# One core, moving-average attention and routed FFN: five half-width jobs made neighbours, steps of copies and stores changed, a sigmoid computed by tanh

## What is computed

```python
def attention(xn):                  # p, a = sigmoid(delta), sigmoid(alpha)
    q = 1 - p * a                   # two decays per feature
    kernel = sum over 2 of p * beta * gamma * (1/2)**0.5 * q**t
    return silu(causal_convolution(xn, kernel) + xn * omega)

def ffn(xn):                        # R = 4 rounds, E = 4 experts, top 2
    cur = xn
    for r in range(4):
        logits = cur @ Wg[r] + bg[r]
        w = softmax of the two highest logits, 0 for the two others
        y_e = gelu(cur @ W1[e] + b1[e]) @ W2[e] + b2[e]      # hidden width 512
        cur = cur + sum_e w_e * y_e
    return cur
```

## Time and profile before

| | us |
|---|---|
| median of 3 executions (lowest, highest) | 658.93 (656.51, 660.35) |
| the profiled execution, its own time | 661.23 |
| its span, first to last instruction | 659.4 |
| PE busy | 604.5 (92%) |
| ACT busy | 515.5 (78%) |
| DVE busy | 474.2 (72%) |
| POOL busy | 395.6 (60%) |
| mean granted clock of TensorE | 0.975 of full speed |

### The profile page before, as it was taken

One profiled execution on the slowest core, in us unless ns is written; L12 is line 12 of the kernel. 1 busy time (PEld: TensorE's weight loads), 2 busy tenths in 40 slices (PEclk: granted clock), 3 DMA queues, 4 the chain that ended last, 5 costly groups with the idle time before them and its releaser, 6 DMA issues.

```text
span 659.4 us, 11311 instructions
## 1 busy us (share of the span) xinstructions
PE 604.5 (92%) x3308; PEld 503.1 (76%) x3308; DVE 474.2 (72%) x1080; ACT 515.5 (78%) x984; POOL 395.6 (60%) x412
## 2 busy tenths in 40 slices
PE   7989999989999999999899999999999999889991
PEld 7767887868877788778787888788877787668780
DVE  4996966588967887559955787659865897647671
ACT  5879688868887789778877888878877788758770
POOL 5665276362875368534864368535868877687154
PEclk8989999989999999999989999999999999989996
DMA  9202033635987489665985589667977688767940
GB/s 243 79 3 64 2 100 105 225 152 219 337 283 254 190 294 351 217 220 225 329 281 210 192 315 347 193 225 271 328 252 266 238 298 303 243 236 282 343 171 32
DMA packets 73754, 146.97 MB, mean 223 GB/s; under 512 B 9383, under 2 KB 37214, under 8 KB 73694
## 3 DMA queue, kind: packets, MB, share of 16 engines
q1 hardware_dynamic: 67396, 134.12, 57.9%
q0 software_dynamic: 5824, 11.87, 5.6%
q10 hardware_dynamic: 474, 0.28, 0.2%
HBM read 37.42 MB, written 12.09 MB: 75 GB/s over the span
## 4 chain that ended last, share of the span: by engine, by line
PE 53%; POOL 15%; DVE 10%; DMA 7%; issue 6%; ACT 4%; SPq 2%; POOLq 0%; DVEq 0%; ACTq 0%
PE z L1479 8%; PE y L1499 7%; PE z L1485 7%; PE z L1482 7%; PE y L1501 7%; PE y L1500 7%; POOL sorted_rows L820 7%; PE spare L1401 5%; DMA w_job<-w_all 4%; POOL state L806 4%; POOL out_dram L837 3%; DVE h_lo L1298 2%; PE misc L1423 2%; ACT z L956 2%; DVE weighted L1226 2%
## 5 line engine op out<-in xcount | busy, mean ns | idle before, releaser
L1298 DVE TENSOR_TENSOR h_lo<-z,h_hi 128x512 fp32r<-128x512 f32 (+1 forms) x432 | 250.0, 592 | 108.1 <-ACT h_hi L959 104.5
L956 ACT ACTIVATE z<-z,w_job 128x512 f32<-128x512 f32 (+1 forms) x368 | 212.9, 579 | 78.4 <-PE z L1485 66.5
L959 ACT CAST h_hi<-z 128x512 fp32r<-128x512 f32 (+1 forms) x432 | 221.8, 513 | 13.7
L806 POOL TENSOR_TENSOR state<-state,weighted 128x512 f32<-128x512 f32 (+1 forms) x90 | 107.0, 1189 | 106.3 <-DVE weighted L1226 105.2
L1479 PE MATMUL z<-cur_hi,w_job 128*128 128x512 f32 (+2 forms) x368 | 138.7, 377 | 6.1 <-DMA w_job<-w_all 5.1
L820 POOL DMA_INDIRECT sorted_rows<-rows,position_i x112 | 115.4, 1031 | 37.0 <-issue 20.9
L1499 PE MATMUL y<-h_hi,w_job 128*128 128x512 f32 (+1 forms) x368 | 131.5, 357 | 4.1 <-DVE h_lo L1298 4.0
L1482 PE MATMUL z<-cur_lo,w_job 128*128 128x512 f32 (+2 forms) x368 | 129.3, 351 | 0.0
L1485 PE MATMUL z<-cur_hi,w_job 128*128 128x512 f32 (+2 forms) x368 | 129.3, 351 | 0.0
L1500 PE MATMUL y<-h_lo,w_job 128*128 128x512 f32 (+1 forms) x368 | 128.9, 350 | 0.0
L1501 PE MATMUL y<-h_hi,w_job 128*128 128x512 f32 (+1 forms) x368 | 128.7, 350 | 0.0
(11 more groups left out here) (165 smaller groups left out, 785.4 us busy)
## 6 DMA issues: line engine op xcount, KB each, us to landing
w_job<-w_all SPq DMA_DIRECT2D x92, 514.5 KB, 3.9
w_job<-w_all SPq DMA_DIRECT2D x92, 512.0 KB, 4.0
gate_bc<-gate_rows SPq DMA_DIRECT2D x71, 256.0 KB
rows<-sorted_rows SPq DMA_DIRECT2D x28, 266.0 KB, 4.3
gate_bc<-gate_rows SPq DMA_DIRECT2D x37, 128.0 KB
out_dram<-x_tok SPq DMA_DIRECT2D x8, 256.0 KB, 5.6
sorted_rows<-rows,position_i POOLq DMA_INDIRECT x112
rows<-in_L_ffn_W_dram SPq DMA_DIRECT2D x4, 256.0 KB, 7.5
```

What stands on the lines that cost most here:

```text
L806: pool.tensor_tensor(state[job.g][:, cols_at], before, weighted[:, j % TR, 0:job.n], ALU.add).then_inc(added, 1)
L956: nc.scalar.activation(zs, zs, ACT.Gelu_apprx_tanh, bias=bias).then_inc(gelu_done, 1)
L959: nc.scalar.copy(h_hi[:, s % ZR, 0:job.n], zs).then_inc(hi_act, 1)
L1298: dve.tensor_tensor(h_lo[:, s % ZR, 0:job.n], zs, hs.bitcast(F32), ALU.subtract).then_inc(lo_done, 1)
```

## The change

1. `SORTED_JOBS`: X3 and X4 stand ahead of F4, so that the five short jobs are fifth to ninth in phases 1 to 6, as they are in phase 7 already.
2. Steps in `SORTED`: transposes, copies and logits around the phase's end, the scatters, the table's parts, the attention parts of the first batch in phases 1 and 2. In `BEFORE_LAST` the stores of group 0.
3. The sigmoids of delta and alpha are 0.5 tanh(0.5 v) + 0.5: ACT's tanh stands behind its first step, the exponential and DVE's reciprocal are gone. The dummy gelu stands first on ACT.
4. ACT's copy of batch 0 out of `spare` stands behind step 0; expert 2's first high part is made by POOL.

```diff
-SORTED_JOBS = "F0 F1 F2 F3 X0 X1 X2 F4 X3 X4 F5 F6 F7".split()
+SORTED_JOBS = "F0 F1 F2 F3 X0 X1 X2 X3 X4 F4 F5 F6 F7".split()
...
-    "P": (42, 45, 51, 53), "P copy": (46, 48, 55, 57), "P split": (44, 46, 49, 55),
-    "P logits": (46, 53, 54, 57), "I": (46, 52, 56, 59), "I copy": (49, 55, 59, 62),
-    "I split": (47, 56, 59, 63), "G": 48, "G copy": 52, "ema": (22, 25, 27, 30, 34, 36), "ema tanh": 36,
-    "A": 41, "A add": 42, ...
-    "places": (17, 18), "pairs": (21, 22), "order": 21, "pick": 28, "jobs": 28, "table": 37,
-    "scatter": (18, 18, 18, 19, 19, 19, 20, 20, 25, 25, 29, 31, 33, 35, 39, 42), "ema 2": (0, 1, 2, 3, 4, 6),
-    "ema tanh 2": 6, "A 2": 7, "A add 2": 10}
+    "P": (42, 44, 51, 53), "P copy": (46, 48, 53, 57), "P split": (44, 46, 49, 55),
+    "P logits": (46, 51, 54, 57), "I": (46, 52, 55, 59), "I copy": (49, 55, 59, 62),
+    "I split": (47, 56, 59, 63), "G": 49, "G copy": 52, "ema": (22, 25, 27, 30, 34, 36), "ema tanh": 36,
+    "A": 39, "A add": 41, ...
+    "places": (17, 18), "pairs": (22, 22), "order": 21, "pick": 27, "jobs": 31, "table": 35,
+    "scatter": (19, 20, 20, 20, 21, 23, 24, 24, 25, 27, 31, 33, 35, 35, 40, 42), "ema 2": (2, 3, 4, 5, 6, 9),
+    "ema tanh 2": 8, "A 2": 11, "A add 2": 14}
...
-    "P add": (43, 46, 53, 57), "finish": (48, 50, 54, 60), "idents": -1,
+    "P add": (43, 46, 53, 57), "finish": (45, 48, 55, 60), "idents": -1,
...
-                    split_weights(e, second, 2 * e + second > 4)
+                    split_weights(e, second, e >= 2)
...
+            act.wait_ge(consts, 2)
+            nc.scalar.activation(warm[:], ident[:, 0:1], ACT.Gelu_apprx_tanh)
             split_weights_hi(0)
             split_weights_hi(1)
-            act.wait_ge(ema_coef_in, 16 * 2)
-            nc.scalar.activation(ema_e[:], ema_in[:, 0:2, :], ACT.Exp, scale=-1.0).then_inc(ema_exp, 1)
-            act.wait_ge(consts, 2)
-            nc.scalar.activation(warm[:], ident[:, 0:1], ACT.Gelu_apprx_tanh)
...
-            act.wait_ge(w1_in[2], 16)
-            nc.scalar.copy(w_all[:, 2, 0:F], w1_raw[:, 2]).then_inc(w_hi, 1)
-            from_spare(("N", 0))
...
+                    if s == 0:
+                        from_spare(("N", 0))
+                        act.wait_ge(ema_coef_in, 16 * 2)
+                        nc.scalar.activation(ema_s[:], ema_in[:, 0:2, :], ACT.Tanh, scale=0.5).then_inc(ema_tanh, 1)
...
-                dve.tensor_scalar(ema_s[:], ema_e[:], 1.0, None, ALU.add).then_inc(ema_chain, 1)
+                dve.tensor_scalar(ema_e[:], ema_s[:], 0.5, 0.5, ALU.mult, ALU.add).then_inc(ema_chain, 1)
                 dve.wait_ge(ema_chain, 1)
-                dve.reciprocal(ema_e[:], ema_s[:]).then_inc(ema_chain, 1)
```

More of the change, by code:

```diff
@@ L118 @@
 SORTED = {
-    "P": (42, 45, 51, 53), "P copy": (46, 48, 55, 57), "P split": (44, 46, 49, 55),
-    "P logits": (46, 53, 54, 57), "I": (46, 52, 56, 59), "I copy": (49, 55, 59, 62),
-    "I split": (47, 56, 59, 63), "G": 48, "G copy": 52, "ema": (22, 25, 27, 30, 34, 36), "ema tanh": 36,
-    "A": 41, "A add": 42, "gates": (7, 8, 8, 10), "tanh": 13, "weights": 15, "count": 16, "ranks": 15,
-    "places": (17, 18), "pairs": (21, 22), "order": 21, "pick": 28, "jobs": 28, "table": 37,
-    "scatter": (18, 18, 18, 19, 19, 19, 20, 20, 25, 25, 29, 31, 33, 35, 39, 42), "ema 2": (0, 1, 2, 3, 4, 6),
-    "ema tanh 2": 6, "A 2": 7, "A add 2": 10}
+    "P": (42, 44, 51, 53), "P copy": (46, 48, 53, 57), "P split": (44, 46, 49, 55),
+    "P logits": (46, 51, 54, 57), "I": (46, 52, 55, 59), "I copy": (49, 55, 59, 62),
+    "I split": (47, 56, 59, 63), "G": 49, "G copy": 52, "ema": (22, 25, 27, 30, 34, 36), "ema tanh": 36,
+    "A": 39, "A add": 41, "gates": (7, 8, 8, 10), "tanh": 13, "weights": 15, "count": 16, "ranks": 15,
+    "places": (17, 18), "pairs": (22, 22), "order": 21, "pick": 27, "jobs": 31, "table": 35,
+    "scatter": (19, 20, 20, 20, 21, 23, 24, 24, 25, 27, 31, 33, 35, 35, 40, 42), "ema 2": (2, 3, 4, 5, 6, 9),
+    "ema tanh 2": 8, "A 2": 11, "A add 2": 14}
 DENSE_PHASE = {
@@ L429, in ema_and_routed_ffn_kernel @@
         wg_ready = sem("wg_ready")
-        ema_exp = sem("ema_exp")
+        ema_tanh = sem("ema_tanh")
         ema_chain = sem("ema_chain")
@@ L1240, in attention @@
                     if c == 0:
-                        dve.wait_ge(ema_chain, 7)
+                        dve.wait_ge(ema_chain, 6)
                     dve.tensor_scalar(pre[:], here, omega_half[:], None, ALU.mult).then_inc(ema_step, 1)
```

7 lines of the change are left out of this document (3 added, 4 removed).

## The result

| | before | changed |
|---|---|---|
| median, us (lowest, highest) | 659.39 (656.51, 660.35), 4 executions | 651.24 (650.07, 651.67), 4 executions |
| profiled execution, span | 659.4 | 649.7 |
| PE busy | 604.5 | 602.8 |
| mean granted clock | 0.975 | 0.981 |

The ratio is 0.9881, with a 95% interval of 0.9847 to 0.9915: faster by 8.1 us, where 10.3 were forecast (648.6 us, range 640 to 657). A second series on another chip gave 651.69 against 658.23 us, ratio 0.9891 (0.9847 to 0.9935).

The account below looks back on a forecast made before the run. PE, busy 604.5 of 659.4 us, was taken as the bound, so gains come only from its idle time and low-clock stretches. Waits removed, less +5.6 for the short jobs and +0.6, summed to -10.3 us: 648.6 us, range 640 to 657.

Parts of the forecast that it names:

- Copies at the phase's end: Starts of phases 2 to 6: PE's five waits on ACT's copies go, -5.8 us, bounds 0 and -5.8.
- End of the dense phase: Later scans give PE its block 2.1 us earlier, leaving a 0.6 us wait without low clock: -3.0 us.
- First batch's attention: Transpose waiting for ACT stands four steps later, -0.7 us; its last DVE part behind the gates costs +0.6.
- State and sorted rows: PE's short waits on X4's add go, -1.4 us; waits on rows read back go if steps between lengthen, -2.5.
- End of phase 6: Wait of 3.66 us on POOL's add goes, wait on x_tok grows from 1.0 to 2.4: -2.3 us.
- Start: ACT reaches its first gelu sooner, so gates from DVE come earlier for PE: -0.8 us, bounds 0 and -1.5.
- Five short jobs in a row: Steps 16 to 40, phases 1 to 6: late weights raise 146.5 to 152.1 us, +5.6; bounds 139.8 and 159.
- The pairs and tables: Pairs, pick, jobs and table parts move among steps with the same DVE work before the same matmul: nothing.
- rival 4: Waits for weights of 1.87 us or more bring low clock in each of six phases: 663.9 us, chance 0.06.
- Rivals 2 and 3: 2: weights come in time, 638.8 us, chance 0.12. 3: PE's waits on ACT's copies move on, 654.4 us, chance 0.15.
- Rival 1: The run of short jobs costs its upper bound, 159 us for steps 16 to 40: 655.5 us, chance 0.15.
- the signs that were named: Predicted PE waits after the change, steps 16 to 40 at 25 to 26 us; wrong if w_job waits exceed 12.

Follow-up runs that it names:

- e9: Kernel before with only the copy of block 2 at step 53 (from 55) and logits of block 1 at 51 (from 53); 654.79 us, ratio 0.9918.
- e10: Changed kernel with an eighth of the weight bytes copied for the five short jobs and F4; 641.88 us, ratio 0.9725; serves for times alone.
- e11: Changed kernel with old job order, block 2's transpose at 56, two gathers at 13 and 14, earlier register loads, first P transposes a step later; 647.87 us, ratio 0.9787.
- e6: Changed kernel with the old order of jobs (F4 between X2 and X3), all table steps as changed; 648.08 us, ratio 0.9855.
- e12: e11 with the last two gathers of phase 6's start at steps 43 and 44 instead of 13 and 14; 645.37 us, ratio 0.9778.
- e4: Changed kernel with the transpose of the next phase's block 2 at step 56 (from 55); ratio 0.9701 on a chip with slower transfers.
- e8: Changed kernel with F4's to F6's register loads read earlier, block 2's transpose at step 56, two phase 6 gathers at 13 and 14; 645.80 us, ratio 0.9831.
- e5: The changed kernel itself again, on another chip; 651.69 us, ratio 0.9891.

## Why the prediction held, and where not

**Copies at the phase's end, -5.8.** Right. All five waits went. e9 measures 4.5 us for it alone (5.4 by the ratio, with an interval of 3.5 to 7.4), and 1.0 us came back there on POOL's adds and 1.0 in phase 6. In the changed kernel, where X4's add comes earlier, nothing comes back on the adds: steps 0 to 8 of phases 2 to 6 lose 2.3 us each and F6 and F7 gain 0.95 in phases 1 to 5, -6.7 together.

**End of the dense phase, -3.0.** Steps 0 to 8 of phase 1 went from 17.43 to 14.34 us (-3.1), and 0.7 of it came back in steps 8 to 16 (10.03 to 10.72), 0.44 of that with the transpose of the first batch's attention, which moved there: -2.4. The low clock is gone. The wait forecast at 0.6 is 1.67, so the step that was wrong is how soon PE starts behind the add. Where it started at once, in e10 and e11, the wait was 0.8 and steps 0 to 8 took 13.5 us, 0.9 less than here.

**First batch's attention, -0.7 and +0.6.** Phase 2 lost 3.65 us in steps 0 to 8 where the phases behind it lost 2.3, and 0.44 came back in steps 8 to 16, again the transpose itself: -0.9. The cost on DVE did not appear.

**State and sorted rows, -1.4 and -2.5.** Both lines are gone from PE's waits. e6 shows the cause for the first: with the old order and the new tables the adds are waited for again, 3.4 us without the dense phase's end. So the order of jobs pays here, not the steps of the scatters. For the second the reason given was wrong: it was to go only if the steps between took longer, yet in e6 they take 146.9 us, as before, and of the 2.5 us only 0.2 are left. PE waits for the adds there instead. In e11 and e12, where the transposes of `P` stand a step later, the waits on the adds are gone and those on the rows are 3.3 and 4.3 us. With the old order one or the other was left in each of these runs. Steps 40 to 52 fell by 2.8 us although 4.7 came in with the logits (0.95 in five phases) and 2.7 of transposes went out; so their waits fell by 4.8, where the two terms had 3.9.

**End of phase 6, -2.3.** The 3.66 us are gone as forecast, but the wait on `x_tok` is 3.12 and not 2.4, since DVE's add to `state` ahead of it takes 1.64 us, where before it took 0.91, and the low clock follows. Steps 0 to 8 of phase 7 fell from 19.99 to 18.21 us: -1.8. It is the transpose at step 55 that costs: with it at 56 the same stretch takes 15.3 us (e4, e8, e11, e12). Some 1.3 us of it is the clock: e6, with the transpose at 55 and a wait of 2.85 us but no low clock behind it, takes 16.46, where e5 takes 18.02 with a wait of 3.12.

**Start of phase 6, not foreseen.** Steps 8 to 16 rose from 11.58 to 13.93 us: +2.35, of it 0.9 with the low clock (13.02 in e5, without it). e9 shows that the gain at the phase's start is enough to bring a part of it (12.60). I had said of a stall that goes that one must name what is late next, and did not do it for POOL's gathers. Their chain came forward by 0.9 us and PE by 2.2, as worked out above at the rows; what PE gains over it turns into waiting for it.

**Start, -0.8.** The pair of profiles shows -1.7. Over 14 profiles the down of step 8 starts at 33.8 to 35.1 us with the old start (four) and at 32.2 to 34.2 with the new one (ten); the means are 34.4 and 33.5, or -0.9. The first gelu comes 1.9 us earlier (13.93 against 15.83), and the tanh of delta and alpha stands between two gelus without a load; the only load is the one at 3.49:

```profile
3.49 1.28 ACT L921 ACT_TABLE_LOAD   x1 [3.49 <-issue]
...
15.10 0.59 ACT L906 COPY xn_T<-spare 128x512 f32<-128x512 f32 x1
15.59 0.21 ACT L958 ACTIVATE ema_s<-ema_in 128x4 f32<-128x4 f32 x1
15.69 0.66 ACT L951 ACTIVATE z<-z,b_all 128x512 f32<-128x512 f32 x1
```

The rule by which the tanh would reload tables did nothing here, as forecast; the prediction had read it into a list that does not say what stands beside this gelu in its own table. Nor is there a pause around the load: the next instruction starts at 4.78, where the load ends.

**Five short jobs in a row, +5.6.** This is the term that was most mis-sized: steps 16 to 40 took 155.9 us and not 152.1, so +9.4 and not +5.6. Of the 3.8 us between them 2.7 are phase 1 with its stretch at the low clock, and 1.1 the five other phases, which took 25.2 to 26.0 us each; for these the price from phase 7, 25.35, was near. The transposes of attention, 2.7 us of PE's work, moved into this stretch, which the working had left out. They do not explain the 9.4: e5 and e6 both have them and differ by 9.4 still. The pairs and tables, booked as nothing, cost about 0.9 us: steps 16 to 24 went from 44.6 to 45.6, with the waits of PE on DVE's `need` up from 2.5 to 3.4 us, and e6 has the same 45.5. The bounds did not hold for each phase. The upper one, 26.5 us a phase, was passed in phase 1, where the wait of 2.09 us brought the low clock: rival 4's mechanism, in one phase of six (in e5 in phase 6, 28.46 us). The lower one, 23.3, for which no row was given, was too low: with an eighth of the weights these steps take 24.3 us or more. In rival 4, 1.87 us was called the shortest wait that the low clock followed; the trace before has one of 1.59 at its start (at 10.86), with the clock low from 12.54. Set against the waits that went with it, the new order of jobs is a loss: e5 and e6 differ by +9.4 and -4.5 us in their steps, where my terms had +5.6 and -3.9.

Together, by the profiles: the terms add up to -10.3. The run (+3.8), the new wait in phase 6 (+2.35), the dense phase's end (+0.6) and phase 6's end (+0.5) are against the forecast, 7.2 us. For it are steps 40 to 52 with the transposes that left them (-3.6), the start, the copies and attention (0.8 to 0.9 each) and the rest of phase 7 (-0.4), 6.7 us. That gives -9.8, as the profiled executions differ (661.23 and 651.44). The medians differ by 8.1. The waits that were to go did go, but that the sum came so near is in part luck, since errors of some 7 us stand on either side. Rivals 2 and 3 did not occur: e10 excludes 139.8 even with few bytes, and no wait on ACT's copies moved on. Rival 1's 159 us was met half-way (155.9, and 156.3 in e5).

Of the signs that were named, the waits on ACT's copies, the 3.66 us, the rows read back and 6.0 us for `w_job` (under 12) came out so. Not so: 1.67 us at the dense phase's end, 3.12 and a low clock instead of 2 to 2.5, and phase 1 outside the 25 to 26 us by two.

## What to carry to other kernels

When PE gains time ahead of an engine that works down a chain of its own (16 indirect transfers of 1.3 us each on POOL), ask at each place where the two meet how much of the gain turns into waiting, and move entries of that chain to where the engine idles: gathers at steps 43 and 44 cost nothing that could be seen, at 8 they cost PE 2.0 us, at 13 and 14 1.9. Short jobs that carry the weights of full ones are better off here with a full job between them: the order that costs PE nothing by its work cost 9.4 us, of which 4.5 came back. An early transpose that is released by a later step's result only moves the wait; one step later it was 2.9 us cheaper where the low clock had followed the wait, and 1.1 where it had not.
